# Two heads at a time in the first two cross attentions: part products, row halves, column quarters

## What is computed

```python
def _L0_xattn_ref(x, context, w_qkv, w_proj, b_proj):      # 16 heads of 8
    qkv = (x @ w_qkv.T).reshape(B, N, 3, H, D).transpose(2, 0, 3, 1, 4)
    q, k, v = (qkv[0], qkv[1], qkv[2])
    kv = context.reshape(B, N_c, 2, H, D).transpose(2, 0, 3, 1, 4)
    extra_k, extra_v = (kv[0], kv[1])
    k = jnp.concatenate([extra_k, k], axis=2)
    v = jnp.concatenate([extra_v, v], axis=2)
    attn = jnp.einsum('bhnd,bhmd->bhnm', q * scale, k).astype(jnp.float32)
    attn = jax.nn.softmax(attn, axis=-1).astype(dtype)
    out = jnp.einsum('bhnm,bhmd->bhnd', attn, v)
    return out.transpose(0, 2, 1, 3).reshape(B, N, C) @ w_proj.T + b_proj

def _L1_xattn_ref(memory, query, seq_mask, b):              # 8 heads of 16
    Q = _split_heads(query, H) * depth ** (-0.5)
    k_mem, v_mem = jnp.split(memory, 2, axis=2)
    logits = jnp.einsum('bhqd,bhkd->bhqk', Q, _split_heads(k_mem, H)) + b[0]
    logits = logits + -1e+30 * (1.0 - mask)
    weights = jax.nn.softmax(logits, axis=-1)
    return jnp.einsum('bhqk,bhkd->bhqd', weights, _split_heads(v_mem, H))
```

## Time and profile before

| | |
|---|---|
| median of 3 runs | 5403.31 us (5402.94 to 5409.03) |
| the profiled execution | 5403.9 us, of which the span of instructions is 5402.1 us |
| busy over the span | PE 86%, DVE 64%, ACT 47%, POOL 25% |
| attention loop of `cross0`, from 179 to 1157 us of the span | 978 us, 128 heads |
| attention loop of `cross1`, from 1551 to 2135 us | 584 us, 64 heads |
| HBM traffic over the span | 27 GB/s |

### The profile page before, as it was taken

One profiled execution on the slowest core, in us unless ns is written; L12 is line 12 of the kernel. 1 busy time (PEld: TensorE's weight loads), 2 busy tenths in 40 slices (PEclk: granted clock), 3 DMA queues, 4 the chain that ended last, 5 costly groups with the idle time before them and its releaser, 6 DMA issues. The chain is left out here.

```text
span 5402.1 us, 94417 instructions
## 1 busy us (share of the span) xinstructions
PE 4622.2 (86%) x30135; PEld 2795.7 (52%) x30135; DVE 3458.3 (64%) x7765; ACT 2525.0 (47%) x4776; POOL 1360.3 (25%) x1426
## 2 busy tenths in 40 slices
PE   3699999977959998658888789999999999999554
PEld 2244444436824444326666456666666666666342
DVE  3577777763256665563333357887878787788546
ACT  3466666642436666313333245555555555555220
POOL 0100000000000000001111036666656656666000
PEclk7899999988979999757777889999999999999657
DMA  4211111100022221000000010000000000000001
GB/s 155 56 46 46 46 52 46 40 17 18 18 72 78 79 78 34 5 18 0 0 0 0 7 49 13 1 13 1 13 13 1 13 1 13 1 1 1 5 4 39
DMA packets 134437, 148.22 MB, mean 27 GB/s; under 512 B 25048, under 2 KB 106552, under 8 KB 133848
## 3 DMA queue, kind: packets, MB, share of 16 engines
q1 hardware_dynamic: 134088, 145.01, 8.9%
q10 hardware_dynamic: 144, 0.52, 0.0%
HBM read 129.85 MB, written 15.66 MB: 27 GB/s over the span
## 5 line engine op out<-in xcount | busy, mean ns | idle before, releaser
L753 DVE TENSOR_REDUCE att_peak.1<-psS 128x1 f32<-128x512 f32 (+1 forms) x1024 | 620.7, 638 | 176.1 <-PE psS L635 146.4
L735 ACT ACTIVATE att_probT.1<-psT 128x512 f32<-128x512 f32 (+1 forms) x1024 | 555.2, 567 | 317.7 <-PE psT L659 312.1
L738 ACT ACTIVATE att_probT.2<-psT,att_key_bias.1 128x256 f32<-128x256 f32 (+1 forms) x832 | 344.8, 471 | 159.4 <-PE psT L661 159.3
L2595 POOL TENSOR_TENSOR key_sums_0.1<-key_sums_0.1,prob_0.1 128x512 f32<-128x512 f32 x256 | 402.3, 1572 | 28.7 <-POOL key_sums_0.1 L2595 0.4
L674 PE MATMUL psM<-att_probT.1,head_values.1 128*32 128x256 f32 (+1 forms) x3840 | 403.5, 391 | 0.1
L2595 POOL TENSOR_TENSOR key_sums_1.1<-key_sums_1.1,prob_1.1 128x512 f32<-128x512 f32 x256 | 386.2, 1509 | 28.7 <-POOL key_sums_1.1 L2595 0.4
L635 PE MATMUL psS<-key_stack.1,query_stack.1 96*128 96x512 bf16 (+1 forms) x1024 | 359.4, 372 | 27.0 <-DMA query_stack.1<-query_parts 25.7
L757 DVE CUSTOM_DVE_ANT_0 att_masked.1<-psS,mask_added.1 128x512 f32<-128x512 f32 (+1 forms) x512 | 290.7, 573 | 135.8 <-issue 129.2
L659 PE MATMUL psT<-query_stack.1,key_stack.1 128*128 128x256 bf16 (+1 forms) x1920 | 360.4, 274 | 12.9 <-ACT query_stack.1 L728 1.0
L2434 ACT COPY prob_0.1<-psS 128x1024 f32<-128x1024 f32 (+1 forms) x224 | 203.7, 954 | 323.2 <-PE psS L2333 323.1
L2434 ACT COPY prob_1.1<-psS 128x1024 f32<-128x1024 f32 (+1 forms) x224 | 203.7, 954 | 296.3 <-PE psS L2333 296.3
(11 more groups left out here) (670 smaller groups left out, 9734.7 us busy)
## 6 DMA issues: line engine op xcount, KB each, us to landing
key_stack.1<-key_parts SPq DMA_DIRECT2D x384, 87.0 KB
key_stack.2<-key_parts SPq DMA_DIRECT2D x128, 150.1 KB
ctx_rows.1<-in_ctx_dram SPq DMA_DIRECT2D x8, 1536.0 KB
key_parts<-split_parts.1 SPq DMA_DIRECT2D x8, 1200.8 KB, 5.7
mask_flags.1<-in_mask_BxS_ik_dram SPq DMA_DIRECT2D x8, 800.5 KB, 6.2
key_stack.2<-key_parts SPq DMA_DIRECT2D x64, 100.1 KB
query_stack.1<-query_parts SPq DMA_DIRECT2D x384, 12.0 KB
ctx_keys_0.1<-in_ctx_dram SPq DMA_DIRECT2D x4, 768.0 KB
```

Of the source, the lines that this page charges most:

```text
L735: last = exp(self.probT[0:w, q % 2, blks[0]:blks[-1] + 1, :].rearrange("p b q -> p (b q)"), self.k.psT[0:w, i % 2, 0:len(blks) * S], ACT.Exp)
L738: last = exp(self.probT[0:w, q % 2, blk, :], self.k.psT[0:w, i % 2, n * S:(n + 1) * S], ACT.Exp, bias=self.bias[0:w, q, blk:blk + 1])
L753: nc.vector.tensor_reduce(self.peak[:, s, c:c + 1], scores, AX_X, ALU.max).then_inc(self.peak_done.sem, 1)
L2595: nc.gpsimd.tensor_tensor(acc, acc, own[:, h, c * BANK:(c + 1) * BANK], ALU.add).then_inc(self.summed.sem, 1)
```

## The change

`ShiftedAttention` and `stage_values` go, and `PairedAttention` comes. What it does:

- Six of the nine part products: key parts (0, 1, 2) with query part 0, (0, 1) with 1 and (0) with 2. In `cross0` that is 48 rows of a head; with the three shift rows a head fits in 64 partitions, and a pair of heads in the two row halves (`halves=True`). In `cross1` 96 rows, three shift rows and three rows of mask parts, which PE adds in the score matmul; each head of a pair has its own stack.
- All loops are over pairs of heads, written out in Python without hardware loops. A slot has the scores of two chunks (two heads), the shifted scores of two heads, and one value block for the four heads of two pairs, one head in each column quarter. Both rings of PSUM banks have three banks, the second `psS` 3 and the two of `psT`.
- One chain of five DVE operations for two heads, one division and one copy of the sums for four heads; two PE transposes take the place of the collecting matmuls.
- The key stack has `RING = 3` places, each for a pair, loaded in 6 copies (8 in `cross1`, with the mask parts). Queries are loaded for four pairs at a time, each row group into two stacks, 24 copies. Two batches' contexts are loaded within the loop rather than before it.
- POOL fills the key stack, two query stacks and the values' tile before the first load, and the shift rows (in `cross1` also the mask rows) once more.
- The masked maximum in `cross1` is a plain one, and the mask of `mask_by_key` is also split in three bf16 parts and stored as `mask_parts`.

```diff
+class PairedAttention:
+    RING = 3
+    SCORE_SLOTS = {8: [[(1, 3)], [(1, 4)], [(1, 5)], [(1, 6)], [(1, 7)], [(2, 0)], [(2, 1)], [(2, 2)]],
+                   7: [[(1, 3), (1, 4)], [(1, 5)], [(1, 6)], [(1, 7)], [(2, 0)], [(2, 1)], [(2, 2)]]}
...
+    def parts(self, h):
+        base = 64 * h if self.halves else 0
+        if self.halves:
+            return [(0, 3, base), (2, 1, base + 24), (1, 2, base + 35)]
+        return [(0, 3, 0), (1, 2, 3 * self.hd), (2, 1, 5 * self.hd)]
...
+    def load_keys(self, sp, g):
+        k = self.k
+        if g >= self.RING:
+            sp.wait_ge(*self.turned(2 * self.NB * (g - self.RING + 1)))
+        loaded = self.keys_loaded[g % self.RING].sem
+        for h in range(2):
+            b, head = self.head(g, h)
+            for _, n, at in self.parts(h):
+                rows = slice(at, at + n * self.hd)
+                sp.dma_start(self.keys(rows, g, h, 0, self.width),
+                             k.key_parts[b, 0:n, head * self.hd:(head + 1) * self.hd, 0:self.width]).then_inc(loaded, 16)
+            if self.masked:
+                sp.dma_start(self.keys(slice(99, 102), g, h, 0, self.width), k.mask_parts[b, :, :]).then_inc(loaded, 16)
+
+    def load_queries(self, sp, f):
+        k, hd = self.k, self.hd
+        if f >= 2:
+            sp.wait_ge(*self.turned(2 * self.NB * 4 * (f - 1)))
+        b, head = self.head(4 * f, 0)
+        heads = k.query_parts[:, head * hd:(head + 8) * hd, b * S:(b + 1) * S].rearrange("j (m a d) n -> j a d m n", a=2, d=hd)
+        for h in range(2):
+            for i, n, at in self.parts(h):
+                for r in range(n):
+                    rows = slice(at + r * hd, at + (r + 1) * hd)
+                    for stack in (self.q_score, self.q_shift):
+                        dst = stack[rows, f % 2] if self.halves else stack[rows, f % 2, :, h, :]
+                        sp.dma_start(dst, heads[i, h]).then_inc(self.queries_loaded[f % 2].sem, 16)
...
+    def sp_run(self, sp, crows):
+        per = self.heads // 2
+        sp.wait_ge(*self.zeroed(self.zeroings))
+        for g in range(self.pairs):
+            if g % 4 == 0:
+                self.load_queries(sp, g // 4)
+            self.load_keys(sp, g)
+            if g == 1:
+                self.load_batch(sp, crows, 0)
+            if g % per == 2 and g // per + 1 < B:
+                self.load_batch(sp, crows, g // per + 1)
...
+    def pe_score(self, pe, g, n):
+        s, c = divmod(n, self.NC)
+        c0, w = self.chunks[c]
+        if n == 0:
+            pe.wait_ge(*self.keys_loaded[g % self.RING](self.key_loads * (g // self.RING + 1)))
+            pe.wait_ge(*self.queries_loaded[g // 4 % 2](self.query_loads * (g // 8 + 1)))
+        for h in range(2):
+            m = 2 * (g * self.steps + n) + h
+            if m >= 3:
+                pe.wait_ge(*self.peak_done(m - 2))
+            rows = self.score_rows(h)
+            self.k.nc.tensor.matmul(self.score_bank[m % 3][:, 0:w], self.queries(self.q_score, rows, g, h, s * P, P), self.keys(rows, g, h, c0, w),
+                                    start=True, stop=True).then_inc(self.score_ready.sem, 1)
...
+    def pe_values(self, pe, q, blk):
...
+        for j in range(4):
+            g, h = 2 * q + j // 2, j % 2
+            last = self.k.nc.tensor.matmul(self.partial[32 * j:32 * j + self.hd + 1, :], self.vquad[0:w, q % 2, blk, j, :],
+                                           self.probT[0:w, g % self.RING, h, blk, :], start=(blk == 0), stop=(blk == self.NK - 1))
+        last.then_inc(self.values_done.sem, 1)
...
+    def pe_run(self, pe):
+        half = -(-self.NK // 2)
+        pe.wait_ge(*self.zeroed(self.zeroings))
+        for g in range(-2, self.pairs + 3):
+            q, odd = divmod(g, 2)
+            for i in range(self.NB):
+                blk = half * odd + i
+                if 0 <= q - 1 < self.quads and i < half and blk < self.NK:
+                    self.pe_values(pe, q - 1, blk)
+                for ahead, n in self.score_slots[i]:
+                    if 0 <= g + ahead < self.pairs:
+                        self.pe_score(pe, g + ahead, n)
+                if 0 <= g < self.pairs:
+                    self.pe_keys(pe, g, i)
+                if i == 1 and odd == 0 and 0 <= q - 2 < self.quads:
+                    self.pe_turn(pe, q - 2, g)
+                if i == self.NB - 2 and 0 <= g + 1 < self.pairs:
+                    self.pe_rows(pe, g + 1)
```

More of the change, by code:

```diff
@@ L611, in over_heads @@
[L611 to L636 removed]
+            sig.passed(2 * self.steps * pairs)
@@ new lines, in queries, with key_loads, query_loads, zeroings @@
+    def queries(self, stack, rows, g, h, at, w):
+        if self.halves:
+            return stack[rows, g // 4 % 2, g % 4, at:at + w]
+        return stack[rows, g // 4 % 2, g % 4, h, at:at + w]
+    @property
+    def key_loads(self):
+        return 16 * (8 if self.masked else 6)
+    @property
+    def query_loads(self):
+        return 16 * 24
+    @property
+    def zeroings(self):
+        return 8 if self.masked else 6
+    @property
+    def stagings(self):
+        return 2 if self.masked else 3
@@ new lines, in pe_keys @@
+            for h in range(2):
+                if n == 0 and m + h >= 3:
+                    pe.wait_ge(*self.exp_done(m + h - 2))
+                rows = self.key_rows(h)
+                last = self.k.nc.tensor.matmul(self.key_bank[(m + h) % 3][0:w, n * S:(n + 1) * S], self.keys(rows, g, h, col, w),
+                                               self.queries(self.q_shift, rows, g, h, 0, S), start=True, stop=True)
+                if n == len(self.bins[i]) - 1:
+                    last.then_inc(self.turned.sem, 1)
@@ L912, in mask_by_key @@
     with ExitStack() as own:
-        mask = k.sb("mask_rows", [B, KC], ctx=own)
+        mask, rest = k.sb("mask_rows", [B, KC], ctx=own), k.sb("mask_rest", [B, KC], ctx=own)
+        parts = k.sb("mask_parts", [B, 3, KC], BF16, ctx=own)
         maskT = k.sb("mask_by_key", [P, B, KB], ctx=own)
```

559 lines of the change are left out of this document (238 added, 321 removed).

## The result

The changed kernel took 5264.43 us (median of 4 runs, 5259.78 to 5283.32), the kernel before 5403.12 us beside it: a ratio of 0.9748 [0.9727, 0.9769], 2.5% faster. The forecast was 5365 us, with 5170 to 5540 as its range: the direction held, the time lies in the range, but the gain is 139 us where 39 were forecast. On the profiled execution (5260.15 us, span 5258.1) it is 143.8 us.

What follows compares the result with a forecast made beforehand. TensorE bound both stages before; afterwards mostly waits for key loads would. Cross0 -100 us and cross1 +61 us, together -39 us on 5403.9 us, gave 5365 us; range 5170 to 5540, the forecast's own 5290 to 5440, chance 0.45.

Steps and rivals of the forecast that it cites:

- The load in series: Both stages: each pair waits one key load, 8.3 us in cross0, 11.8 in cross1, in series with its last three slots.
- rival B: Both attention loops: key loads hidden, engines bound at 10.3 and 11.2 us a pair; -436 us, 4968 us; chance 0.15.
- The queries: SP's queue: 24 query copies ahead of keys make SP late, 60 us over 15 cross0 pairs, 20 us over 7 in cross1.
- The three slots of cross0: Cross0, slots 5 to 7 on PE behind the key wait: 3.5 us a pair, added to the 8.3 us load.
- The clock: TensorE slows after key waits: 1.5 us for each cross1 pair and each of 15 cross0 pairs, 22 us in cross0.
- rival C: Clock at 0.50 behind each cross1 key wait, queries at 0.74 us: slower, 5573 us together; chance 0.25.
- Cross1: Cross1's loop: 32 pairs of 17.4 us, plus 20 for queries and 22 to fill and drain: 599 for 583, +16 us.
- The starts: Before each stage's first score: longer POOL fills, query copies ahead of keys; cross0 17 us later, cross1 41.
- D: Cross0 scores and keys: row halves don't overlap in bf16, 58 us more, 5423 us; chance 0.15.

Runs made afterwards that it cites:

- The doubled copies: Each query copy sent as two of half its rows, 48 for four pairs instead of 24, against the changed kernel: 5437.07 us, +166 us.

## Why the prediction was right in its signs and too small

**The load in series: right.** Landings of 8.32 and 12.02 us stood against 8.3 and 11.8, TensorE's waits for the keys, 1.6 and 3.7 us a pair, against 2 and 4. A fourth place took them away, and brought the pairs to 10.9 and 12.0 us on average, for the 10.3 and 11.2 that rival B had worked out for the engines.

**The queries: the step that failed.** The forecast said that no row has this form, bounded a copy by 0.38 and 0.74 us, took 0.50, and made SP 4.0 us late 15 times, 60 us. The row that it cited for 8 rows had 0.33 us; with the gap a copy takes 0.345, below the lower bound. SP is then done 12.6 us after its first key, against a pair of 11.6: about 1 us late. In the trace it issues these keys 1.0 us after the key matmuls that it waits for, on average from the ninth pair on (0.03 us in the other pairs), and the pairs behind queries are 1.1 us longer (12.69 for 11.59), 16 us in all. This is 44 of the 86 us. A difference of two near numbers was multiplied by 15, so 0.155 us a copy became 3.7 us a time. The doubled copies bore out the mechanism. In cross1 0.62 was taken for 0.47: SP needs 15.9 us (4.6 + 24 x 0.47) of a pair's 18.0, and the term of 20 us was nothing.

**The three slots of cross0: a second term too high.** The forecast took 3.5 us for the slots from the first score to the next key issue. At the full clock they took 3.0, which is 31 us over 63 pairs. The load was 8.2 us from the ninth pair on for 8.3.

**The clock: there in both stages, at another size.** In cross1 the three slots took 6.4 us and 4.0 with TensorE kept at work: 2.4 us a pair, where the forecast had 1.5 and rival C 4.1. The Trainium skill (TensorE: Matmul & The Clock Gate, HAM oscillation) describes such bursts between waits for DMA, and the trace agrees, with 0.50 behind the waits and 0.73 over the stage, just below the 0.75 to 0.95 forecast. In cross0 the forecast put 1.5 us on each of the 15 pairs with queries, 22 us. The slots behind the wait were slow in 18 of 42 pairs that have no queries behind them, and the cost is 0.4 us a pair, some 25 us. That the sum came out near is in part luck, since the dips fall on pairs of every kind and cost far less in each than 1.5 us.

A cross0 pair without queries is thus 8.2 + 3.0 + 0.4 = 11.6 us, as measured (11.59). With the forecast's clock spread over all its pairs it had 11.8 + 22 / 63 = 12.15, 35 us more in 63 pairs. The end of the loop took 30 us for 36. Queries, pairs and end make up cross0's loop: 44 + 35 + 6 = 85 of the 86 us.

**Cross1** came out within 5 us in the loop, two errors of opposite sign in it: no queries (-20), and pairs of 17.97 us for 17.4 (+18). From the ninth pair on they average 18.5, since the clock takes 2.4 us and not 1.5; that the errors cancel is luck. The starts were 13.5 and 34.1 us later for 17 and 41, by the query copies (8.3 us for 12 and 11.3 for 15) and in cross1 by the fills, 31.9 us for 34.3.

**The rivals.** B (loads hidden) did not hold for the change, and holds with a fourth place. C's mechanism is there, in cross1 at 2.4 of its 4.1 us, and did not decide: its price of a query copy, 0.74 us, was the further from the 0.345. D is out: two scores in separate halves took 0.39 us together, and matmuls in one half stood one behind the other.

## What to carry to other kernels

When a ring is made of larger places, count how many it has in time, not in places: here three pairs took the place of four heads, a place came free only once a pair, and every load stood in series with three slots; a fourth place was worth 237 us, more than the whole change. Where a queue's work is nearly as long as the iteration that hides it, the price of one issue decides; take it from the row with the same rows per copy. Try single parts in place of one copy of three as well: it gave 170 us here, for the same bytes and more issues. And where filler work is used to find what the clock costs, look at the slots behind the wait and not at the total: in cross0 the total moved by 3 us in the trace while the slots gave 0.4 us a pair, and the filler took it back.

## What was not expected of the hardware

- The time that SP's queue needs for a copy hardly goes by its bytes: 0.34 us for 4 rows of queries and for 8, and 0.34 for 8 rows of keys sent alone, with 29 KB; 0.47 for 16; 0.69 to 0.79 for key copies of two or three parts.
- A fill costs by its columns alone, on VectorE as on POOL: 4.70 and 4.74 us for 5571, whether 3 rows or 128.
- In the run traced, TensorE's granted clock stayed at 0.50 (1.2 GHz) through 1334 us in which it was busy for 1332, when the bf16 scores and keys of cross0 all stood in one row half; with both halves in use it was 0.92 over the stage, waits included. Whether the halves or the order of the matmuls made the difference was not tried.
